# Projecting cross-attention's first queries, keys and values among self-attention's last jobs

## The chip, the cores and the metric

The kernel runs on one core of a Trainium2 chip. A core has TensorE for matrix products (PE in the profile, with its weight loads as PEld), VectorE (DVE), ScalarE (ACT), GpSimd (POOL), SyncE (SP), which here issues nearly all transfers, and 16 DMA engines. Each engine works through its own instructions in order, and semaphores order the engines among each other. The metric is the device time of one execution in microseconds. The kernel before took 792.21, 797.68 and 798.51 us in three runs, with a median of 797.68 us.

## The reference

It is a decoder layer for 8 batches of 256 tokens with 512 channels in fp32. Three sublayers follow one another, and each adds its result to its input:

```
x = x + attn(layernorm(x), w_qkv, w_out)          # 16 heads of 32 channels, causal softmax
x = x + xattn(layernorm(x), ctx, wq, wk, wv, wo)  # one head of 512 channels
x = x + ffn(layernorm(x), wg, W, b)               # 8 experts, the best one for each token

# cross-attention: the keys and values are the context and, behind it, the new tokens
q, k_new, v_new = x @ wq.T, x @ wk.T, x @ wv.T
k = concat([ctx, k_new]);  v = concat([ctx, v_new])        # 512 keys for 256 queries
out = softmax(q @ k.T / sqrt(512)) @ v @ wo.T
```

## The kernel before

**Exact products from rounded parts.** The kernel splits each fp32 operand into a high part and a low part (the rest), both in the type fp32r. A product is three passes over four chunks of 128 channels (`three_pass`, L50 to L61): high by high, low by high and high by low, so twelve matmuls. ScalarE usually writes the high part (a cast), and VectorE subtracts it from the source to get the low part. GpSimd splits some weights too.

**Three stages, one after the other.** `self_attention`, `cross_attention` and `mixture_of_experts` each open a block of their own. A block ends when all engines have finished it. Semaphores, buffers and PSUM banks of a stage belong to its block.

**Self-attention** walks over batches n = 0 to 7, and each batch has 16 slots, one for each head. Every engine has a function `slot(n, h)` with its share of slot h, and the software pipeline is written as lags: in slot h, the scores of head h are reduced, head h-1 is rounded, head h-2 is transposed by a DMA, and the values product of a group of four heads comes 7 slots after its last head. The chain of one head is: scores (PE, four heads at once), maximum (VectorE L613), shift (GpSimd L337), exponential (ScalarE L411), high part (GpSimd L344), low part (VectorE L621), DMA transpose (SP L258). Beside the heads, `SLOTS` places jobs of TensorE: X0 and X1 (transposes of the normalized input of the next batch, slot 8), y0 and y1 (the output product of the batch before, slots 10 and 11, L60 with 512 columns), q0, k0, q1, k1 of the next batch (slots 12 to 15), q2, k2, q3, k3 (slots 0 to 3), and the halves u0, u1, w0, w1 of the values (slots 4 to 7). Each job has ScalarE write the high part in its slot (L398) and VectorE the low part one slot later (L592). Jobs share three PSUM banks. For the values, VectorE writes a rest `v_rest` instead, and GpSimd makes two more parts of it (L311, L313, waits `v_mid_done` and `v_done`). In the function `values`, TensorE waits for `v_done` before the first pass of groups 0 and 2. In `evac`, VectorE waits until the rest buffer of two jobs ago is free.

There is no batch 8. So in n = 7 the slots 8 and 12 to 15 have no jobs for a next batch, and after slot 15 a tail n = 8 follows in which only lagged work is left: transposes of the last heads, the values of groups 2 and 3, then y0 and y1 for batch 7.

**Cross-attention** runs a list of jobs for each batch: `X0 X1 s0 s1 q0 q1 p0 p1 q2 q3 o0 o1 o2 o3 k0 y0 y1 k1 k2 k3 v0 Y0 Y1 v1 l0 l1` (L859), where X, q, k and v are for the next batch and the others for this one. TensorE may run up to seven PSUM banks ahead. So that batch 0 has its operands, a prologue runs first: X0 X1 q0 q1 q2 q3 k0 k1 k2 k3 v0 v1, together with the layernorm of batch 0, the split of wq and wk on ScalarE and VectorE (L1032, L1219, eight pieces each of 128 columns), the split of wv and wo on GpSimd (L986, L988) and that of the context. After the prologue TensorE waits for wo's split and for the routing constants before X0 of batch 0.

The weights of cross-attention, and its queries, keys, values and probabilities, lie in the places of the eight experts' weights, which mixture_of_experts fills at the end (`PLACES`). Self-attention has buffers of its own for all of that. wq and wk are loaded into `stage[0]` and `stage[1]` at the start of the kernel; wv, wo and the context are loaded at the start of cross-attention.

Of the kernel before, what the change touches and what calls it, by code (L numbers as in the profile page):

```python
# [20 lines left out]
P = 128  # L21
B, S, D = 8, 256, 512
DC = D // P
# [41 lines left out]
def self_attention(nc, ident, x, w_qkv, w_out, x1, xin, xr, x1_out, x1_last_out, x1_first_in,  # L65
                   stage, stage_in, next_weights):
# [8 lines left out]
    with ExitStack() as cx:  # L75
# [3 lines left out]
        w_hi, w_lo = sb("wqkv_hi", [P, DC, 3 * D], F32R), sb("wqkv_lo", [P, DC, 3 * D], F32R)  # L79
        wo_hi, wo_lo = sb("wout_hi", [P, DC, D], F32R), sb("wout_lo", [P, DC, D], F32R)  # L80
        stats, mv = sb("a_stats", [P, TB, 6]), sb("a_mv", [P, TB, 2])
        veps, rstd, expo = sb("a_veps", [P, TB]), sb("a_rstd", [P, TB]), sb("a_expo", [P, TB])
        xn = sb("a_xn", [P, TB, D])
        xt_hi, xt_lo = sb("a_xt_hi", [P, DC, S], F32R), sb("a_xt_lo", [P, DC, S], F32R)


        q_part = [sb(f"q_part{i}", [P, G, S], F32R) for i in range(2)]
        k_part = [sb(f"k_part{i}", [P, G, S], F32R) for i in range(2)]

        v_part = [sb(f"v_part{i}", [P, TB, D], BF16) for i in range(3)]  # L90
        v_rest = sb("v_rest", [P, TB, D // 2])
# [8 lines left out]
        ot_hi, ot_lo = sb("ot_hi", [P, G, S], F32R), sb("ot_lo", [P, G, S], F32R)  # L100
        raw = sb("a_raw", [P, 4, DC, D])
# [19 lines left out]
        on_done, ot_hi_done, ot_done = sem("on_done"), sem("ot_hi_done"), sem("ot_done")  # L121

# [19 lines left out]

        def piece_columns(piece):
            i = "qkuw".index(piece[0])
            if piece in "uw":
                return 2, slice(2 * D + (i - 2) * D // 2, 2 * D + (i - 1) * D // 2)
            return i, slice(i * D + int(piece[1]) * P, i * D + (int(piece[1]) + 1) * P)

        def raw_columns(piece):
            i, cols = piece_columns(piece)  # L150
            return raw[:, i, :, cols.start - i * D:cols.stop - i * D]

        def has(j, n):

            if not isinstance(n, int):
                return True
            return n >= 1 if j in LATE else n < B - 1 if j in NEXT else n < B
# [69 lines left out]
        def parts_of(j, n):  # L227

            b, i = bank(j), int(j[1])
            if j[0] == "X":  # L230
                cols = slice(i * P, (i + 1) * P)
                return xt_hi[:, :, cols], xt_lo[:, :, cols], b[:, :].rearrange("p (c n) -> p c n", c=DC)
            if j[0] in "uw":
                return v_part[0][:, i, v_half(j)], v_rest[:, i, :], b[:, 0:D // 2]
# [6 lines left out]
        def _(sp):  # L241
            sp.dma_start(xin[:], batch_rows(x, 0)).then_inc(x0_in, 16)
            for i, w in enumerate([w_qkv[:, j * D:(j + 1) * D] for j in range(3)] + [w_out]):
                sp.dma_start(raw[:, i, :, :], w.rearrange("(c p) n -> p c n", p=P)).then_inc(w_in[i], 16)
# [3 lines left out]
            for i, w in enumerate(next_weights):  # L248
                sp.dma_start(stage[i][:], w.rearrange("(c p) n -> p c n", p=P)).then_inc(stage_in[i], 16)
# [10 lines left out]

            def slot(n, h):
                if h == 13 and not (isinstance(n, int) and n in (0, B)):
                    sp.wait_ge(job_ev, job_at("y1", n) + 1)
                    sp.dma_start(batch_rows(x1, n - 1), xr[:]).then_inc(x1_out, 16)
                if h == 1 and not (isinstance(n, int) and n < 2):
                    sp.wait_ge(x1_out, (n - 1) * 16)
                    sp.dma_start(xr[:], batch_rows(x, n - 1)).then_inc(xr_in, 16)
                if h == 7 and (not isinstance(n, int) or n < B - 2):
                    sp.wait_ge(xn_ready, (n + 2) * TB)
                    sp.dma_start(xin[:], batch_rows(x, n + 2)).then_inc(x_in, 16)  # L270
                if h == 7 and isinstance(n, int) and n == B - 1:
                    sp.wait_ge(x1_out, 16)
                    sp.dma_start(xin[:], batch_rows(x1, 0)).then_inc(x1_first_in, 16)
                if head_at(h, DMA_LAG, n) is not None:
                    transpose(h, n)
# [1369 lines left out]
```

## Time and profile before

| what | value |
|---|---|
| three runs | 792.21, 797.68, 798.51 us (median 797.68) |
| the profiled execution's own time | 792.9 us |
| its span in the trace | 791.1 us |
| mean granted TensorE clock | 0.935 of full |
| busy over the span | PE 87%, DVE 63%, ACT 39%, POOL 41% |
| self-attention's block | 0 to 332.7 us |
| cross-attention's prologue | 333.5 to 363.5 us |
| cross-attention's batches | 363.5 to about 680 us |

The span is the time from the first to the last instruction in the trace. A row of the timeline has the start, the time from the first to the last of the merged instructions, the engine and line, what is written and read, how many were merged, and in brackets the idle time of the engine before it with what ended that idle time. PEclk is the granted clock as a share of the full one.

### The profile page before, as it was taken

To read this page: it belongs to the slowest core of one execution; us is meant where nothing else is said; L and a number is where in the kernel's file an instruction comes from. 1 tells how busy PE (TensorE), PEld (TensorE's weight loads), DVE (VectorE), ACT (ScalarE), POOL (GpSimd) and SP (SyncE) were. 2 spreads that over 40 slices of the span, in tenths; PEclk is the share of its full clock that TensorE was granted. 3 is DMA by queue.
4 is the path that set the end of the run, shared out by engine and by line. 5 is a ranking of instruction groups with operands and counts; after the bars stand their busy time and mean duration, and the time that the engine had idled before them with its cause. 6 is when DMAs were issued, how large, how long until landed. Compare 5 with 4: busy or idle time off the path is not lost. (4 is left out here: it accounts for less than half of the span.)

```text
span 791.1 us, 19082 instructions
## 1 busy us (share of the span) xinstructions
PE 684.9 (87%) x6040; PEld 610.1 (77%) x6041; DVE 502.4 (63%) x1454; ACT 307.1 (39%) x982; POOL 321.5 (41%) x538
## 2 busy tenths in 40 slices
PE   4769999999999995588999999999999986239995
PEld 4759888888989884487988888888888976228884
DVE  4778787877878766286645464646464557626663
ACT  3446656666656654133231222222222343102220
POOL 4396766667575756153000101010101046436662
PEclk9889999999999998679999999999999998559998
DMA  9365865766556576195312222222222046346530
GB/s 341 98 108 83 136 150 115 144 133 125 133 115 144 116 142 139 53 327 205 115 46 82 79 80 80 80 80 80 80 80 80 11 122 187 80 137 185 184 119 16
DMA packets 142885, 95.07 MB, mean 120 GB/s; under 512 B 110846, under 2 KB 115070, under 8 KB 142720
## 3 DMA queue, kind: packets, MB, share of 16 engines
q1 hardware_dynamic: 137184, 82.00, 40.7%
q0 software_dynamic: 5664, 12.61, 5.2%
q8 instruction: 19, 0.31, 0.2%
q14 instruction: 18, 0.15, 0.1%
HBM read 56.14 MB, written 18.77 MB: 95 GB/s over the span
## 5 line engine op out<-in xcount | busy, mean ns | idle before, releaser
L411 ACT ACTIVATE prob<-prob,shift 128x128 f32<-128x128 f32 (+1 forms) x256 | 114.6, 449 | 116.0 <-POOL shift L337 115.4
L60 PE MATMUL b_bank<-w_hi 128*128 128x256 f32 (+1 forms) x576 | 119.9, 331 | 7.1 <-DVE w_lo L1204 7.1
L1016 ACT CAST w_hi<-b_bank 128x256 fp32r<-128x256 f32 (+1 forms) x144 | 60.3, 446 | 160.9 <-PE b_bank L60 142.9
L60 PE MATMUL b_bank<-w_lo,w_hi 128*128 128x256 f32 (+1 forms) x576 | 114.9, 322 | 0.0
L60 PE MATMUL b_bank<-w_hi,w_lo 128*128 128x256 f32 (+1 forms) x576 | 114.6, 322 | 0.0
L60 PEld LDWEIGHTS b_bank<-w_hi 128*128 128x128 f32 x576 | 90.1, 196 | 15.6 <-DVE w_lo L1204 7.7
L613 DVE CUSTOM_DVE_ANT_0 prob<-a_s,mask 128x128 f32<-128x128 f32 (+1 forms) x256 | 79.6, 347 | 30.6 <-PE a_s L489 30.5
L1204 DVE TENSOR_TENSOR w_lo<-b_bank,w_hi 128x256 fp32r<-128x256 f32 (+1 forms) x144 | 68.3, 507 | 47.5 <-ACT w_hi L1016 47.4
L60 PEld LDWEIGHTS b_bank<-w_lo,w_hi 128*128 128x128 f32 x576 | 90.8, 195 | 8.0
L60 PEld LDWEIGHTS b_bank<-w_hi,w_lo 128*128 128x128 f32 x576 | 90.7, 194 | 7.6
L621 DVE TENSOR_TENSOR p_part<-prob,p_part 128x384 f16<-128x384 f32 x128 | 77.1, 602 | 8.2 <-POOL p_part L344 7.0
L337 POOL TENSOR_SCALAR shift<-nmax 128x2 f32<-128x2 f32 x128 | 41.6, 325 | 88.7 <-DVE nmax L613 84.9
L344 POOL CAST p_part<-prob 128x384 f16<-128x384 f32 x128 | 64.5, 504 | 8.8 <-ACT prob L411 0.7
L60 PE MATMUL a_job<-a_xt_hi,wqkv_hi 128*128 128x256 f32 x256 | 45.7, 302 | 9.4 <-DVE k_part L592 4.0
L512 PE MATMUL a_o<-pt,v_part 128*32 128x128 f16 (+1 forms) x1280 | 33.8, 254 | 20.1 <-DMA pt<-p_part 10.4
L972 POOL TENSOR_TENSOR b_rstd<-b_veps,b_expo 128x2 f32<-128x2 f32 x8 | 6.1, 758 | 109.5 <-DVE b_veps L1182 109.5
L411 ACT ACTIVATION_READ_ACCUMULATOR prob<-prob,shift 128x1 f32 x256 | 48.2, 188 | 0.0
L60 PEld LDWEIGHTS a_job<-a_xt_hi,wqkv_hi 128*128 128x128 f32 x256 | 35.6, 196 | 13.8 <-DVE k_part L592 5.6
L512 PEld LDWEIGHTS a_o<-pt,v_part 128*32 128x32 bf16 x1280 | 26.0, 99 | 25.5 <-issue 22.1
L976 POOL TENSOR_TENSOR b_rstd<-b_veps,b_expo 128x2 f32<-128x2 f32 x8 | 5.6, 699 | 95.7 <-DVE b_veps L1182 95.6
L1485 ACT CAST c_xt_hi<-c_bank 128x512 fp32r<-128x512 f32 x23 | 13.5, 588 | 74.6 <-PE c_bank L1505 74.6
L60 PE MATMUL a_job<-a_xt_lo,wqkv_hi 128*128 128x256 f32 x256 | 41.7, 287 | 0.0
(171 smaller groups left out, 1377.0 us busy)
## 6 DMA issues: line engine op xcount, KB each, us to landing
stage<-in_w SPq DMA_DIRECT2D x8, 1024.0 KB, 5.4
xin<-in_x SPq DMA_DIRECT2D x8, 512.0 KB, 4.3
xr<-in_x SPq DMA_DIRECT2D x8, 512.0 KB, 4.3
x<-xr SPq DMA_DIRECT2D x8, 512.0 KB, 3.2
xin<-x SPq DMA_DIRECT2D x8, 512.0 KB, 4.5
b_cin_t<-in_ctx_t SPq DMA_DIRECT2D x8, 512.0 KB, 3.5
b_cin<-in_ctx SPq DMA_DIRECT2D x8, 512.0 KB, 3.6
xr<-x SPq DMA_DIRECT2D x8, 512.0 KB, 4.5
```

Of the source, the lines that this page charges most:

```text
L60: ins = pe_matmul(out, a, b, start=first and i == 0, stop=last and i == len(steps) - 1)
L337: nc.gpsimd.tensor_scalar(shift[:, e, :], nmax[:, e, :], LN_UNIT, None, ALU.add).then_inc(shift_done, 1)
L344: nc.gpsimd.tensor_copy(p_part[:, t % NPROB, 0, :], prob[:, t % NPROB, :]).then_inc(p_hi_done, 1)
L411: a = nc.scalar.activation(prob[:, e % NPROB, cols], prob[:, e % NPROB, cols], ACT.Exp, scale=-1.0, bias=shift[:, e, q:q + 1], accum_out=r ...
L512: m = nc.tensor.matmul(o_ps[j * HD:(j + 1) * HD, 0, seen], v_part[a][:, k, at:at + HD], pt[:, (g * HG + j) % NPT, 3 * z + blocks.start:3 * ...
L613: m = nc.vector.tensor_tensor_reduce(out=prob[:, s % NPROB, cols], in0=s_ps[s % HG][:, q, 0:P * (q + 1)], in1=mask[:, P * (1 - q):], scale ...
L621: nc.vector.tensor_tensor(p_part[:, t % NPROB, 1, :], prob[:, t % NPROB, :], p_part[:, t % NPROB, 0, :], ALU.subtract).then_inc(p_done, 1)
L972: nc.gpsimd.tensor_tensor(rstd[:, 0, :], veps[:, 0, :], expo[:], ALU.pow).then_inc(ln_rstd, 1)
L976: nc.gpsimd.tensor_tensor(rstd[:, 1, :], veps[:, 1, :], expo[:], ALU.pow).then_inc(ln3_rstd, 1)
L1016: nc.scalar.copy(hi, src).then_inc(job_hi, 1)
L1204: nc.vector.tensor_tensor(lo, src, hi.bitcast(F32), ALU.subtract).then_inc(job_ev, 1)
L1485: nc.scalar.copy(xt_hi[:, k % 2, :], t_ps[k % 2][:, :]).then_inc(xt_hi_done, 1)
```

## The change

1. **Jobs.** The slots that were empty in n = 7 and in the tail now carry cross-attention's work for its batch 0. X0 and X1 transpose the normalized output of self-attention's batch 0. The table `CROSS` says which product stands in which slot: q0 to q3 in slots 12 to 15 of n = 7, k0 to k3 in slots 0 to 3 of the tail, v0 and v1 in slots 4 and 5 of the tail. The prologue of cross-attention is gone, and so are its waits.
2. **Weights.** wq, wk and wv are split in twelve pieces of 128 columns among the slots of n = 6 and n = 7 (`NEXT_PIECES`): ScalarE writes all high parts, GpSimd the even and VectorE the odd low parts. The context of batch 0 is split in the tail (`CTX_SLOTS`). Cross-attention splits only wo.
3. **Norms.** The layernorms of cross-attention's batches 0 and 1 are done in n = 7 and in the tail, from loads of x1 in slot 7.
4. **Places.** Self-attention's weights and operands now lie in the experts' places too: w_qkv in 3, 2 and 5, w_out in 7, queries and the transposed input in 4, keys and output in 6. Its raw weights go to the three `stage` buffers, so w_out, wk and wv are loaded in slots 2 and 3 of batch 0, behind waits, and wq in slot 0 of batch 1.
5. **Values.** `v_rest` has four places, so VectorE waits for a rest two jobs later than before. TensorE waits for `v_mid_done` before the passes, and for `v_done` only before the last pass.
6. **Loops.** VectorE, ScalarE and GpSimd leave their loop one batch earlier, and n = 6 is written out.
7. **SP.** In slot 1 the load of xr is issued after the transpose and not before it. In slot 9 of n = 7 two loads of the context stand before the transpose.

```diff
+        CROSS = {(B - 1, "q0"): "q0", (B - 1, "k0"): "q1", (B - 1, "q1"): "q2", (B - 1, "k1"): "q3", (B, "q2"): "k0",
+                 (B, "k2"): "k1", (B, "q3"): "k2", (B, "k3"): "k3", (B, "u0"): "v0", (B, "u1"): "v1"}
+        NEXT_PIECES = {**{(B - 2, 2 * i + 1): i for i in range(2 * DC)}, **{(B - 1, 2 * i + 5): 2 * DC + i for i in range(DC)}}
+        CTX_SLOTS = {(B, 0): 0, (B, 1): 1}
...
             def slot(n, h):
+                if isinstance(n, int) and (n, h) == (0, 2):
+                    sp.wait_ge(w_split, PIECES.index("q3") + 1)
+                    sp.dma_start(raw[3], chunks(w_out)).then_inc(w_in[3], 16)
+                if isinstance(n, int) and (n, h) == (0, 3):
+                    sp.wait_ge(w_split, PIECES.index("k3") + 1)
+                    load_next(1)
+                    sp.wait_ge(wv_split, 2)
+                    load_next(2)
+                if isinstance(n, int) and (n, h) == (1, 0):
+                    sp.wait_ge(wo_split, DC)
+                    load_next(0)
...
+                if h == 9 and isinstance(n, int) and n == B - 1:
+                    wait_next_split(sp, DC)
+                    sp.dma_start(ctx_t_raw, chunks(ctx_t[0:D, :])).then_inc(ctx_in, 16)
+                    sp.dma_start(ctx_raw, batch_rows(ctx, 0)).then_inc(ctx_in, 16)
...
+                i = at_slot(NEXT_PIECES, n, h - 1)
+                if i is not None and i % 2 == 0:
+                    next_low(nc.gpsimd, i)
...
-                if g == 0:
-                    pe.wait_ge(v_done, v_at("u1", of) + 1)
-                if g == G // 2:
-                    pe.wait_ge(v_done, v_at("w1", of) + 1)
+                first_use = {0: "u1", G // 2: "w1"}.get(g)
+                if first_use:
+                    pe.wait_ge(v_mid_done, v_at(first_use, of) + 1)
...
                 for a, z in PASSES:
+                    if first_use and a == 2:
+                        pe.wait_ge(v_done, v_at(first_use, of) + 1)
...
-                if j[0] in "uw":
-                    wait(dve, v_done, v_at(j, n) - 1)
+                if j[0] in "uw" and not crossed(j, n):
+                    wait(dve, v_done, v_at(j, n) - 3)
```

In cross_attention, SP and then TensorE:

```diff
-            sp.dma_start(raw[2][:], chunks(wv)).then_inc(w_in[2], 16)
-            load_ctx_t(0)
-            sp.dma_start(raw[3], chunks(wo)).then_inc(w_in[3], 16)
-            sp.dma_start(cin[:], batch_rows(ctx, 0)).then_inc(c_in, 16)
+            load_ctx_t(1)
+            sp.dma_start(wo_raw, chunks(wo)).then_inc(wo_in, 16)
+            sp.dma_start(cin[:], batch_rows(ctx, 1)).then_inc(c_in, 16)
...
-            for j in PROLOGUE:
-                job(j, -1)
-            pe.wait_ge(wg_in, 16)
-            pe.wait_ge(wo_split, 2)
-            pe.wait_ge(routing.consts, Routing.CONSTS)
```

The wait for wo's split now stands before y0 of batch 0, and those for wg and for the routing constants before its l0.

## Rows read from the trace of the kernel before

**Rows 1.** The page: busy time, share of the span and instructions of each engine.
```profile
PE 684.9 (87%) x6040; PEld 610.1 (77%) x6041; DVE 502.4 (63%) x1454; ACT 307.1 (39%) x982; POOL 321.5 (41%) x538
```
**Rows 2.** Windows: steady self-attention, its tail, the prologue, cross-attention's batch 0.
```profile
core 0: us, PE busy (x) PEld busy (x) DVE busy (x) ACT busy (x) POOL busy (x), PEclk, DMA share, GB/s
303.40:332.70 29.30, 16.73 (x181) 12.83 (x180) 10.09 (x30) 6.34 (x23) 7.96 (x16) 0.65 0.33 78
332.70:363.50 30.80, 21.43 (x128) 19.73 (x129) 25.90 (x36) 11.48 (x22) 18.43 (x18) 0.83 0.83 278
363.50:403.50 40.00, 39.74 (x256) 36.45 (x257) 20.76 (x45) 11.14 (x24) 1.40 (x2) 0.96 0.40 145
232.84:268.55 35.71, 34.12 (x449) 30.44 (x449) 28.86 (x111) 21.96 (x87) 23.46 (x50) 1.00 0.56 118
```
**Rows 3.** Timeline of the tail: last scores, values of groups 2 and 3, y.
```profile
303.40 0.96 PE L489 MATMUL a_s<-k_part,q_part 32*128 32x128 f32 x24
311.84 1.79 PE L512 MATMUL a_o<-pt,v_part 128*32 128x256 f16 x40 [5.90 <-DMA pt<-p_part]
321.03 1.22 PE L519 MATMUL a_o<-ident,rinv_wide 128*128 128x128 f32 x4
323.67 2.08 PE L60 MATMUL a_job<-wout_hi,ot_hi 128*128 128x512 f32 x4 [1.41 <-ACT ot_hi L419]
330.89 1.08 PE L60 MATMUL a_job<-wout_hi,ot_lo 128*128 128x512 f32 x4
```
**Rows 4.** Timeline: the first instruction of VectorE in the new block, X0 of batch 0.
```profile
333.69 1.28 DVE L1176 BATCH_NORM_STATS2 b_stats<-xin 128x6 f32<-128x512 f32 x2 [0.99 <-PEq L75]
363.53 1.94 PE L1105 MATMUL b_bank<-ident,b_xn 128*128 128x128 f32 x8 [2.93 <-issue]
365.12 1.89 PE L60 MATMUL b_bank<-w_hi 128*128 128x512 f32 x4
```
**Rows 5.** Timeline of one steady batch, TensorE: scores, values, X, y, scores.
```profile
232.84 0.96 PE L489 MATMUL a_s<-k_part,q_part 32*128 32x128 f32 x24
249.87 0.96 PE L489 MATMUL a_s<-k_part,q_part 32*128 32x128 f32 x24
259.08 1.09 PE L462 MATMUL a_job<-ident,a_xn 128*128 128x128 f32 x8
261.46 1.01 PE L512 MATMUL a_o<-pt,v_part 128*32 128x256 f16 x40 [1.29 <-POOL v_part L313]
262.86 1.18 PE L60 MATMUL a_job<-wout_hi,ot_hi 128*128 128x512 f32 x4
268.55 0.96 PE L489 MATMUL a_s<-k_part,q_part 32*128 32x128 f32 x24
```
**Rows 6.** TensorE's waits from 64 to 300 us: total, times, longest.
```profile
PE a_o L512 <- POOL v_part L313: 8.6, 7, 1.3
```
**Rows 7.** The same batch on GpSimd and ScalarE, around y0.
```profile
260.02 1.09 POOL L313 TENSOR_TENSOR v_part<-v_rest,v_part 128x256 bf16<-128x256 f32 x1
262.33 0.39 ACT L419 CAST ot_hi<-a_o_sb 128x256 fp32r<-128x256 f32 x1
```
**Rows 8.** By line: GpSimd's low part of 128x512 (min/median/max ns).
```profile
L321 POOL TENSOR_TENSOR wout_lo<-a_raw,wout_hi x4: 1288/1447/1466, 44.8 to 59.5; 128x512 fp32r<-128x512 f32 x4
```
**Rows 9.** Prologue: GpSimd's low part of a weight, VectorE meanwhile, L1219's min/median/max ns.
```profile
343.78 4.64 POOL L988 TENSOR_TENSOR w_lo<-stage,w_hi 128x2048 fp32r<-128x2048 f32 x1
344.51 0.43 DVE L1204 TENSOR_TENSOR w_lo<-b_bank,w_hi 128x256 fp32r<-128x256 f32 x1 [2.83 <-ACT w_hi L1016]
L1219 DVE TENSOR_TENSOR w_lo<-stage,w_hi x8: 676/681/3942, 335.4 to 350.2; 128x512 fp32r<-128x512 f32 x8
```
**Rows 10.** Batch 0 of cross-attention: the context's low part, y0; and wo's transfer.
```profile
374.37 1.22 DVE L1213 TENSOR_TENSOR w_lo<-b_cin_t,w_hi 128x1024 fp32r<-128x1024 f32 x1 [1.78 <-ACT w_hi L1026]
385.60 1.16 PE L60 MATMUL b_bank<-w_hi 128*128 128x512 f32 x4 [0.23 <-DVE w_lo L1204]
bias_sb<-in_wo SPq DMA_DIRECT2D x1, 1024.0 KB, 10.1
```

More of the change, by code:

```diff
@@ L61, in three_pass, with cross_views, self_attention @@
     return ins
-def self_attention(nc, ident, x, w_qkv, w_out, x1, xin, xr, x1_out, x1_last_out, x1_first_in,
-                   stage, stage_in, next_weights):
+CROSS_PLACES = {"q": 0, "k": 1, "v": 2, "o": 6}
+def cross_views(experts):
+    views = {n: experts.place(e) for n, e in CROSS_PLACES.items()}
+    views.update(kt=experts.place(3), xt=experts.place(4, 0, S), qt=experts.place(4, S, D), values=experts.place(5),
+                 pt=experts.place(7, 0, S), ot=experts.place(7, S, D))
+    return views
+def self_attention(nc, ident, x, w_qkv, w_out, x1, xin, xr, xn, x1_out, x1_last_out, stage, stage_in, next_weights,
+                   ctx, ctx_t, experts):
     scale = float(HD) ** -0.5
@@ L99, in self_attention @@
         o_sb = [sb(f"a_o_sb{i}", [P, S]) for i in range(2)]
-        ot_hi, ot_lo = sb("ot_hi", [P, G, S], F32R), sb("ot_lo", [P, G, S], F32R)
-        raw = sb("a_raw", [P, 4, DC, D])
+        ot_hi, ot_lo = experts.place(6, S, D)
+        raw = [stage[i][:] for i in (0, 1, 2, 0)]
+        ctx_raw = stage[0][:, 2:4, :]
+        ctx_t_raw = stage[0][:, 0:2, :].rearrange("p a n -> p (a n)").rearrange("p (c s) -> p c s", c=DC)
         job_ps = [ps(f"a_job{i}", [P, D]) for i in range(3)]
@@ L884, in route_after @@
             return "q3" if order(n) is ORDER else "p1"
[L886 to L887 removed]
         def bank(j, n):
[L890 to L893 removed]
+            return ring[order(n).index(j) % RING]
         def parts_of(j, n):
@@ L1076, in wait_bank @@
             def wait_bank(j, n):
-                before = jobs_in(n).index(j) - RING
+                before = order(n).index(j) - RING
                 if before >= 0:
-                    last, of = jobs_in(n)[before], n
-                elif isinstance(n, int) and n < 0:
+                    last, of = order(n)[before], n
+                elif isinstance(n, int) and n < 1:
                     return
@@ L1084, in wait_bank @@
                     of = n - 1
-                    there = len(jobs_in(of))
-                    last = jobs_in(of)[max(i for i in range(there) if i % RING == before + RING)]
+                    there = len(order(of))
+                    last = order(of)[max(i for i in range(there) if i % RING == before + RING)]
                 if last[0] == "s":
```

351 lines of the change are left out of this document (177 added, 174 removed).

## The prediction

> **What bounds the kernel now.** I read the busy shares first, then windows by stage, then TensorE's waits and timeline where its share falls. Over the whole span TensorE is busy 87% [rows 1], but the windows part this [rows 2]: 34.12 of 35.71 us in a steady batch of self-attention and 39.74 of 40.00 in batch 0 of cross-attention, yet only 16.73 of 29.30 in self-attention's tail and 21.43 of 30.80 in the prologue. TensorE sets the pace in the long stages. The 60 us between them go by chains, at a granted clock of 0.65 and 0.83. The timeline of the tail shows why [rows 3]: after the last scores at 303.40, TensorE waits 5.90 us for transposed probabilities, then the values come at half pace, and y0 starts at 323.67. The last of y1 ends at 331.97. The first new work of the next block starts at 333.69, and X0 of batch 0 only at 363.53 [rows 4]. So 31.6 us lie between the end of self-attention on TensorE and batch 0. The chain of waits ends in the experts' stage, which is not touched; its work follows when batch 0 starts earlier.
>
> **The prologue and the tail.** All twelve jobs leave the stretch before 363.53. Two go to slot 8 of n = 7, ten behind the last scores. To size the new tail I lay a steady batch over it. There the stretch from scores of group 3 to those of group 1 takes 249.87 - 232.84 = 17.03 us [rows 5]; it holds four jobs of the kind q and k in slots 12 to 15, values of groups 1 and 2, and four more jobs in slots 0 to 3, just what the new tail has. It also holds the scores of group 0 (0.96 us by the row of scores), which the tail has not: 16.1. The jobs v0 and v1 have 512 columns as y has: y0 and y1 together take 268.55 - 262.86 = 5.7 us, so v0 and v1 take 5.7 too. Values of group 3 take 1.4 (261.46 to 262.86). Then comes the chain from the end of the reciprocals' product to y0, 323.67 - (321.03 + 1.22) = 1.4 [rows 3], and y0 and y1, 5.7. The sum is 30.3, against 331.97 - 303.40 = 28.6 before. **The tail is only 1.7 us longer although ten jobs moved in**: they fill the wait of 5.90 and the wait for group 3, and they keep the clock up, so that the values and y0 no longer take double. Adding the 1.7 us from the last matmul to the next block (331.97 to 333.69), X0 of batch 0 would start at 331.97 + 1.7 + 1.7 = 335.4 in place of 363.53: **-28.1 us**.
>
> For this the transposed probabilities must be there in time. Before, group 2's came at 311.84 and group 3's before the reciprocals' product at 321.03 [rows 3]; TensorE would now ask for them about 12 and 22 us after the last scores, at 315 and 325. They are hidden. What is late next is the evacuation of the jobs: three banks, ScalarE and VectorE also with the context's parts (two of 1.22 us on VectorE [rows 10]) and a norm. VectorE was busy 10.09 us of the 29.30 in the tail [rows 2] and gets about 9 more (ten low parts of 0.43 [rows 9] or above, the context's 2.4, the norm as an estimate 2.5). I take **+1**, with bounds 0 and +4 (all three new large pieces of about 1.3 us in front of one evacuation).
>
> X0 and X1 in slot 8 of n = 7 cost 1.1 us. In steady batches TensorE waits there for the values' parts anyway, 8.6 us in 7 times [rows 6]. I put them at nothing; without that cover they would cost 1.1.
>
> **The clock at batch 0.** X0 and X1 ran 1.94 us and the first four matmuls of s0 1.89, after an idle time of 2.93 [rows 4]; at the full clock the same shapes take 1.09 and 1.08 [rows 3, 5] (the row of X, and the last four matmuls of y1). In the new kernel TensorE pauses about 1.7 us. An idle time of 1.29 in the steady batch left y0 at full pace [rows 5]. That row is nearer: **-1.7**, bounds -1.7 and 0.
>
> **Splitting twelve pieces during n = 6 and n = 7.** ScalarE has 13.8 us idle in a batch, VectorE 6.9, GpSimd 12.3 [rows 2]. GpSimd gets six low parts of 1.45 us [rows 8], VectorE six of 0.68 [rows 9]. Over a batch this fits. But one piece of GpSimd falls in slot 6 of each of the two batches, among the values' parts, and GpSimd's order there leads to y0: the second part of u1 (260.02 to 261.11), then the shift of head 8, the exponential, ot_hi (262.33 to 262.72), y0 at 262.86 [rows 5, 7]. The slack is 0.14 us, so each piece there costs 1.3. The others meet idle time of GpSimd, but can hold VectorE. I take **+3** (twice 1.3, and 0.4), bounds 0 and +8 (all six at 1.45 in the path, 8.7, less some).
>
> **The values' waits.** The edit takes away nearly all of the 8.6 us [rows 6], since `v_mid_done` comes 1.09 us before `v_done`. It would be -8.6 if nothing else came last. But y0, which follows, waits for ot_hi, and that ends 0.14 us before y0 starts [rows 5, 7]; GpSimd's work ahead of it is unchanged. So a wait for ot_hi takes the place of the one removed. Seven times 0.14 is **-1**; bounds -9.6 (all eight waits, the one in batch 0 with them) and +1 (the second wait between passes).
>
> **Batch 0 of cross-attention.** y0 comes 385.60 - 363.53 = 22.1 us after X0 [rows 10, 4]. wo's transfer landed 10.1 us after its issue [rows 10] with 1 MB more ahead of it, which at the prologue's 278 GB/s [rows 2] is 3.8 us; GpSimd's low part takes 4.64 [rows 9], its cast by my estimate half of that, and the issue comes some 2 us into the block: 2 + 10.1 - 3.8 + 2.3 + 4.6 = 15.2, or 19 without the 3.8. y0 is covered. The danger is GpSimd's low part itself. In the prologue GpSimd's first one ran from 343.78 to 348.42. VectorE's low parts of weight pieces, from SBUF like it, took 0.68 us in the middle and once 3.94, in that time; one with a source in PSUM took only 0.43 [rows 9]. Before, that fell in the prologue. Now it starts some 10 to 14 us after X0, and the context's low part starts 10.8 us after X0 [rows 10]; the low parts of q and p queue behind it on VectorE, and o0 waits for p's. If it loses, o0 is 4 us late. The Trainium skill ("SBUF — State Buffer", section "SBUF: two separate sides") says that VectorE with two SBUF inputs and GpSimd take a shared port pair as an exclusive lock for a whole instruction, the first one winning. The trace agrees (3.94 us). I take half, **+2**, bounds 0 and +4.6.
>
> **The start.** w_out, wk and wv (3 MB) leave the kernel's first transfers and come in slots 2 and 3, wk and wv ahead of the transposes of heads 1 to 3 on SP's queue. Their 2 MB take some 7 us by the prologue's 278 GB/s [rows 2], so some transposes can land up to 7 us late; the values of their group stand in slot 10, five slots on. w_out's first piece was split at about 44 us [rows 8], long after slot 2. The Trainium skill ("DMA: Bandwidth & Descriptors", "Queues, rings and completion order") has each DMA engine take its descriptors in ring order; that rule would put the whole 7 us in front of the transposes, and the sum would then be 4 us higher if GpSimd had to wait for the buffers. I take **+1**, bounds -1 and +5. The new places, the written-out batch and the later xr load I put at nothing: cross-attention's matmuls already read the same places with TensorE busy 39.74 of 40.00 us [rows 2], and xr is needed only in slot 10.
>
> **The sum**: -28.1 + 1 - 1.7 + 3 - 1 + 2 + 1 = -23.8. The profiled execution took 792.9 us, so 769.1. The runs' median is 797.68, 4.8 above this execution, and the lowest run 0.7 below; I forecast **770**.
>
> **Rivals.** *The values' waits come off whole*: if the order of parts lets ot_hi move up with them, self-attention is another 7.6 us shorter, 761.5. For it speaks that VectorE no longer stalls twice a batch on the same parts; against it the 0.14 us. Chance 0.16. *The locks spread*: the six pieces of GpSimd stop it and VectorE one after the other (2 x 1.45 x 6 = 17.4 in place of 3), and batch 0 loses 4.6 in place of 2: 769.1 + 14.4 + 2.6 = 786. Against it is the idle time of both engines. By the SBUF page's lock this is the outcome when GpSimd always wins; the one row that shows it has a POOL instruction three times as long. Chance 0.12. *Nothing is hidden in the tail* (the change doesn't do what it says): the evacuations and the context make the ten jobs follow one another behind the last values. Their work, eight of 1.4 and 5.7, is 17 us, in place of 1.7 and 1: 769.1 + 14.3 = 783. Against it are the 12.6 us that TensorE idles there [rows 2]. Chance 0.08. *Slower*: the wait between the passes. TensorE now holds inside `values` until GpSimd's last part, in every batch, while VectorE, freed of its waits, takes the shared ports from GpSimd with its p_part instructions. If each of the eight batches loses 3.6 us or more, the 28.8 lost are more than the 28.6 between 769.1 and the median, and at 5 us it is 809. For it speaks that the part already takes 1.09 us [rows 7] beside VectorE, against it that it would have to take four times as long. Chance 0.03.
>
> **How the numbers follow.** The forecast has 0.61. Its own range is 762 to 777. For 8 in 10 I take in the first rival with what the unknown costs allow below and most of the second and third: 757 to 785. A change under 1% (8 us) can't be told from none here. Faster by over 1% (under 789.7) is the forecast, the first rival, and most of the second and third: 0.92. Within 1%: the upper ends of those two, 0.05. Slower: 0.03.
>
> **What would show it.** In the changed profile, X0 of cross-attention's batch 0 should start at about 333 to 340 us, with PEclk near 1 in the tail and no wait for transposed probabilities over 1 us. The last scores of n = 7 should come at 303 to 308. The wait for L313 should be gone and one for ot_hi stand there, at the same period of 35.7 us. Batch 0 should take 38 to 43 us, with a VectorE instruction of about 4 us beside GpSimd's low part if the lock is met. I am wrong if the steady period moves by over 1 us, or if the tail is over 36 us long.

## The result

The changed kernel took **762.08 us** (median of 4 runs, 761.97 to 764.43) beside 797.98 us (792.21 to 798.51) for the kernel before: a ratio of 0.957, with a 95% interval of 0.953 to 0.962 (intervals stand behind the ratios below too). Run again later it took 761.31 us beside 789.24, a ratio of 0.965 (0.962 to 0.969); the two intervals hardly touch, and the difference lies in the kernel before, whose median was 789.2 to 790.6 us in the three later sets of runs. Both are faster, and both agree on the kernel after. The forecast was 770, range 757 to 785. The drop is 36 us in the first set and 28 in the second. The two profiled executions differ by 28.4 us in their spans (791.1 and 762.7), and it is these 28.4 us that can be followed place by place. The executions themselves took 792.9 and 764.43.

The page of the kernel after: the span, busy time by engine, and the granted clock in 40 slices.

```profile
span 762.7 us, 18978 instructions
PE 677.9 (89%) x6040; PEld 604.5 (79%) x6041; DVE 497.5 (65%) x1452; ACT 309.2 (41%) x986; POOL 322.2 (42%) x542
PEclk9969999999999999999999999999999988559998
```

TensorE's work is nearly what it was [rows 1], and its share rose by two points because the span shrank. The hole of low clock between the two stages is gone. Its own windows, which answer to [rows 2], are the new tail, batch 0 of cross-attention, and a steady batch of self-attention (columns as there):

```profile
312.31:342.70 30.39, 28.78 (x301) 25.04 (x300) 18.30 (x49) 13.24 (x40) 12.58 (x21) 1.00 0.38 81
...
344.38:383.20 38.82, 38.28 (x256) 35.13 (x257) 22.91 (x44) 11.03 (x24) 10.83 (x16) 1.00 0.90 316
201.11:236.86 35.75, 34.80 (x449) 30.97 (x449) 29.09 (x111) 22.00 (x87) 23.18 (x50) 1.00 0.61 132
```

The tail now keeps TensorE busy for 28.78 of 30.39 us at the full clock, where it had 16.73 of 29.30 at 0.65. Its timeline answers to [rows 3] and [rows 4]:

```profile
316.27 1.01 PE L632 MATMUL a_o<-pt,v_part 128*32 128x256 f16 x40
...
324.07 1.01 PE L632 MATMUL a_o<-pt,v_part 128*32 128x256 f16 x40
...
333.99 1.01 PE L632 MATMUL a_o<-pt,v_part 128*32 128x256 f16 x40
334.93 0.71 PE L639 MATMUL a_o<-ident,rinv_wide 128*128 128x128 f32 x4
337.06 1.20 PE L60 MATMUL a_job<-w_hi 128*128 128x512 f32 x4 [1.41 <-ACT w_hi L516]
...
344.38 1.06 PE L1190 MATMUL b_bank<-ident,xn 128*128 128x128 f32 x8 [1.59 <-PEq L89]
345.19 1.17 PE L60 MATMUL b_bank<-w_hi 128*128 128x512 f32 x4
```

No values product waits for transposed probabilities any more, each takes 1.01 us in place of 1.79, and X0 of the next block takes 1.06 in place of 1.94. The only wait over 1 us in the tail is the one for the rounded output (w_hi of L516 is `ot_hi`) ahead of y0, 1.41 us, the same as before.

**Where the 28.4 us are.** I read the start of the last scores (group 3) of each batch of self-attention, and of X0 of each batch of cross-attention, in both timelines, and took differences:

| stretch | before | after | difference | forecast |
|---|---|---|---|---|
| start to last scores of n = 0 | 48.69 | 52.66 | +3.97 | +1 |
| n = 1 to 5 | 184.15 | 184.20 | +0.05 | -1 (seven waits) |
| n = 6 and 7 | 70.56 | 75.45 | +4.89 | +3 |
| last scores to X0 of batch 0 | 60.13 | 32.07 | -28.06 | -27.1 |
| batch 0 | 40.03 | 38.82 | -1.21 | +0.3 (-1.7 and +2) |
| X0 of batch 1 to X0 of batch 6 (five periods) | 201.06 | 191.41 | **-9.65** | 0 |
| after the last X0 | 186.48 | 188.09 | +1.61 | 0 |

The sum is -28.40. The forecast of -23.8 is near it, but two errors cancel in part: a gain of 9.65 us that it did not have at all, and 4.9 us more loss at the start and in n = 6 and 7 than it had. With the missed gain left out, the change made the execution 18.75 us shorter and not 23.8.

Each column is one execution. The places before cross-attention hang on it by about 1 us: in the mirror experiment below, self-attention's code is that of the kernel before, and its last scores of n = 0 came at 49.34 us in place of 48.69 and its batches 1 to 5 took 183.00 in place of 184.15, a steady period of 35.50 and not 35.71. Differences under about 1 us in the table mean nothing by themselves.

### The profile page after: what moved, and what is told of

Read it like the earlier page. It is cut to its first block and busy times, and to the rows that moved or that the text cites. A ratio compares the mean times of both kernels' runs of the same rounds, so it can differ in the third digit from the quotient of the medians.

```text
span 762.7 us, 18978 instructions
## 1 busy us (share of the span) xinstructions
PE 677.9 (89%) x6040; PEld 604.5 (79%) x6041; DVE 497.5 (65%) x1452; ACT 309.2 (41%) x986; POOL 322.2 (42%) x542
## 5 line engine op out<-in xcount | busy, mean ns | idle before, releaser
L60 PE MATMUL b_bank<-w_hi 128*128 128x256 f32 (+1 forms) x536 | 109.7, 327 | 3.2 <-DVE w_lo L1281 3.2
L60 PE MATMUL a_job<-w_hi 128*128 128x256 f32 (+1 forms) x488 | 94.5, 317 | 15.0 <-DVE w_lo L711 7.2
L60 PE MATMUL b_bank<-w_hi,w_lo 128*128 128x256 f32 (+1 forms) x536 | 106.8, 322 | 0.0
L60 PE MATMUL b_bank<-w_lo,w_hi 128*128 128x256 f32 (+1 forms) x536 | 106.7, 322 | 0.0
L60 PEld LDWEIGHTS a_job<-w_hi 128*128 128x128 f32 x488 | 71.3, 195 | 24.8 <-DVE w_lo L711 7.8
L60 PE MATMUL a_job<-w_lo,w_hi 128*128 128x256 f32 (+1 forms) x488 | 87.7, 303 | 0.0
L60 PE MATMUL a_job<-w_hi,w_lo 128*128 128x256 f32 (+1 forms) x488 | 87.1, 301 | 0.0
L60 PEld LDWEIGHTS a_job<-w_lo,w_hi 128*128 128x128 f32 x488 | 72.3, 195 | 3.0
L60 PEld LDWEIGHTS a_job<-w_hi,w_lo 128*128 128x128 f32 x488 | 72.2, 195 | 2.9
L711 DVE TENSOR_TENSOR w_lo<-a_job,w_hi 128x256 fp32r<-128x256 f32 (+1 forms) x92 | 43.2, 477 | 18.8 <-ACT w_hi L495 18.4
```

Of the source, the lines that this page charges most:

```text
L60: ins = pe_matmul(out, a, b, start=first and i == 0, stop=last and i == len(steps) - 1)
L711: nc.vector.tensor_tensor(lo, src, hi, ALU.subtract).then_inc(job_ev, 1)
```

## The experiments

### The gain that was not forecast: the order of two loads

The edit puts back the order in which SyncE issues its loads in a batch of cross-attention:

```diff
                 if load:
+                    sp.wait_ge(ct_split, n + 1)
+                    load_ctx_t(n + 2)
                     if not (isinstance(n, int) and n == 0):
                         sp.wait_ge(xn_ready, n * TB)
                         sp.dma_start(xin[:], batch_rows(x1, n + 2)).then_inc(x_in, 16)
-                    sp.wait_ge(ct_split, n + 1)
-                    load_ctx_t(n + 2)
```

> The changed kernel with one thing put back: in cross-attention's batches, SP again issues the load of the next-but-one x1 rows (xin) behind the load of the transposed context and not ahead of it. Theory A (VectorE's wait for xin set 1.5 us of each cross-attention batch): X0 to X0 goes from 38.3 to about 39.75 us in batches 1 to 5, VectorE shows waits of 3.2 us for xin again, and TensorE waits before the ranks; in all 7 to 11 us longer, about 771. Rival B (the cross-attention batches became shorter for another reason, the places or the time at which the experts' weights arrive): 762 to 764, and X0 to X0 stays at 38.3.

It took 772.34 us (ratio 0.978, 0.974 to 0.982). The mirror experiment makes the same edit, turned round, in the kernel before, and nothing else:

```diff
-                    sp.wait_ge(ct_split, n + 2)
-                    load_ctx_t(n + 2)
                     sp.wait_ge(xn_ready, (n + 2) * TB)
                     sp.dma_start(xin[:], batch_rows(x1, n + 2)).then_inc(x_in, 16)
+                    sp.wait_ge(ct_split, n + 2)
+                    load_ctx_t(n + 2)
```

> The kernel before with that one part of the change alone: SP issues the xin load of a cross-attention batch ahead of the wait for the context's split. Theory A: the batches fall from 39.75 to about 38.3 us, batch 1 with its 41.8 by more, in all 8 to 11 us, so 788 against 798. Rival B: no change, 796 to 799.

It took 780.82 us beside 790.48 for the kernel before, 9.7 less (ratio 0.988, 0.983 to 0.992). The five periods from X0 of batch 1 to X0 of batch 6 sum to 201.31 us with the late load in the changed kernel and to 191.27 us with the early one in the kernel before; the two kernels themselves have 201.06 and 191.41. So the order of the loads carries the 9.65 us whole, in either kernel, and the rest of the change none of it.

The rows show how. First the kernel before, SyncE's queue in one batch, then VectorE in the same batch:

```profile
495.88 0.37 SPq L914 DMA_DIRECT2D b_cin_t<-in_ctx_t  x1
496.51 0.37 SPq L945 DMA_DIRECT2D xin<-x  x1
```

```profile
494.48 1.23 DVE L1213 TENSOR_TENSOR w_lo<-b_cin_t,w_hi 128x1024 fp32r<-128x1024 f32 x1 [1.78 <-ACT w_hi L1026]
...
500.86 1.29 DVE L1176 BATCH_NORM_STATS2 b_stats<-xin 128x6 f32<-128x512 f32 x2 [3.22 <-DMA xin<-x]
```

The load of xin stands behind a wait for VectorE's split of the context (494.48 to 495.71). It is issued at 496.51 and wanted by VectorE only a little later: VectorE stands for 3.22 us, and the low parts behind it stand too. In the kernel after, SyncE has already issued xin when it comes to that wait, and VectorE's row has no wait:

```profile
472.21 1.27 DVE L1256 BATCH_NORM_STATS2 b_stats<-xin 128x6 f32<-128x512 f32 x2
```

What TensorE waits for from X0 of batch 0 to the end, before and after (total us, times, longest; the experts' stage and its DMA left out):

```profile
PE b_bank L60 <- DVE w_lo L1204: 5.8, 7, 1.6
PE r_ranks L731 <- DVE r_onehot L716: 5.1, 6, 1.8
```

```profile
PE b_bank L60 <- DVE w_lo L1281: 3.2, 3, 1.6
...
PE r_ranks L857 <- DVE r_onehot L842: 1.7, 1, 1.7
```

VectorE was busy 22.09 of 39.75 us in such a batch, and still set 1.5 us of it, by one wait. Of these 1.5 us TensorE spent 1.05 waiting; for the other 0.4 it was busy longer with the same 263 matmuls. In the kernel before, two batches in a row (X0 to X0 of batch 1, and of batch 2), and one of the kernel after:

```profile
403.56:445.37 41.81, 40.04 (x263) 36.69 (x263) 22.14 (x58) 10.85 (x25) 3.58 (x4) 0.96 0.26 76
...
445.37:485.12 39.75, 38.70 (x263) 35.33 (x263) 22.09 (x58) 10.85 (x25) 3.87 (x6) 1.00 0.24 79
```

```profile
421.49:459.76 38.27, 38.27 (x263) 35.25 (x263) 22.31 (x58) 11.13 (x25) 3.86 (x6) 1.00 0.38 83
```

TensorE no longer waits in such a batch. In batch 1 of the kernel before the waits came with a clock of 0.96, which made its work 1.3 us longer besides.

### The start: bulk loads ahead of the transposes

In the kernel after, GpSimd waits for a transpose in batch 0, which it never did before, and SyncE's queue shows what stood ahead of it (the second fence: start, length, what was issued):

```profile
POOL p_part L426 <- DMA pt<-p_part: 4.1, 1, 4.1
```

```profile
31.84 0.57 SPq L324 DMA_DIRECT2D stage<-in_wk  x1
32.46 0.51 SPq L324 DMA_DIRECT2D stage<-in_wv  x1
33.08 9.49 SPq L320 DMA_TRANSPOSE pt<-p_part  x4
```

The experiment moves both loads into batch 1:

```diff
-                if isinstance(n, int) and (n, h) == (0, 3):
+                if isinstance(n, int) and (n, h) == (1, 5):
                     sp.wait_ge(w_split, PIECES.index("k3") + 1)
                     load_next(1)
+                if isinstance(n, int) and (n, h) == (1, 9):
                     sp.wait_ge(wv_split, 2)
                     load_next(2)
```

> The changed kernel with the loads of wk and wv moved from slot 3 of batch 0 to slots 5 and 9 of batch 1. Theory A (the 4 us lost at the start are GpSimd's wait of 4.1 us for transposes that stand behind these 2 MB): the last scores of batch 0 come at 48.7 and not 52.7 us, and 758 in all. Rival B (the start is late because the splits come from other buffers or w_out lands late): the scores stay at 52 to 53 us, 762. Rival C (the 2 MB cost the same wherever they stand): 762, with the 4 us lost in batch 1.

It took 759.64 us (ratio 0.961, 0.957 to 0.965; the kernel after has 0.957 and 0.965 in its two sets of runs). The last scores of batch 0 came at 48.78 in place of 52.66, so the start's loss is due to these two loads. But those of batch 1 came at 93.30 in place of 93.91: batch 1 took 44.52 us in place of 41.25. TensorE's waits in that batch show the load's cost again, in a new place:

```profile
PE a_s L609 <- issue: 5.2, 3, 4.4
PE a_o L633 <- DMA pt<-p_part: 2.9, 1, 2.9
...
```

In this execution the third theory held: the transfers cost about the same in batch 1 as in batch 0. But it took 761.91 us, the longest of the four runs; the others took 758.05 to 759.71, between the first theory's 758 and the third's 762, and have no trace. So how often the cost comes back is not shown, and the last kernel below shows that it need not.

### Batches 6 and 7: does the place of the pieces matter?

```diff
-        NEXT_PIECES = {**{(B - 2, 2 * i + 1): i for i in range(2 * DC)}, **{(B - 1, 2 * i + 5): 2 * DC + i for i in range(DC)}}
+        NEXT_PIECES = {**{(B - 2, h): i for i, h in enumerate((1, 3, 4, 6, 8, 10, 12, 14))},
+                       **{(B - 1, h): 2 * DC + i for i, h in enumerate((4, 6, 8, 11))}}
```

> The changed kernel with the twelve weight pieces at other slots: GpSimd's now fall in slots 2, 5, 9 and 13 of n = 6 and 5 and 9 of n = 7, and no longer in slots 6 and 10, where it also makes the values' parts. Theory A (a piece costs about 1.3 us where GpSimd's parts lead to y0, and nothing elsewhere): of the 4.9 us that n = 6 and n = 7 lost, 2 to 3 come back, 759 to 760. Rival B (the cost is the shared work on all engines, wherever it stands): 761 to 763.

It took 760.34 us (ratio 0.962, 0.958 to 0.966). Batches 6 and 7 took 38.66 and 37.26 us, 75.92 together, against 75.45 in the kernel after (75.45 to 75.50 in the five executions whose n = 6 and 7 have the code of the kernel after). My theory, that two pieces in slot 6 of GpSimd cost 1.3 us each and the others next to nothing, is refuted. In both kernels the loss is about 5 us, and in both TensorE waits for GpSimd's first part of the values (L394, L395) again, which it does not do in the steady batches of the kernel after. Here are the waits, the kernel after first:

```profile
PE a_o L632 <- POOL v_part L394: 2.5, 2, 1.4
PE a_job L60 <- ACT w_hi L516: 2.2, 2, 1.1
```

```profile
PE a_o L633 <- POOL v_part L395: 2.7, 2, 1.9
PE a_job L60 <- DVE w_lo L712: 1.0, 2, 0.8
PE a_job L60 <- ACT w_hi L517: 0.6, 1, 0.6
```

Not all of the 4.9 us is waiting. TensorE was busy 70.07 us of these 75.45, and 67.50 of 70.56 before: 2.6 us are longer work, 2.3 are waits. About 0.9 of the work is X0 and X1: n = 7 took 34.85 us before, without them, where a batch with them takes 35.71 [rows 2]. Most of the rest is an effect that the steady batches show too: 449 matmuls keep TensorE busy 34.80 us there in place of 34.12 [rows 2], and steady batches hide it in their waits (next section). The waits are not tied to a slot of the pieces. No run leaves the pieces out, and n = 7 also got the norms and loads for cross-attention, so that the waits come from the pieces at all is argued and not shown.

### The values' waits: what gives them back

```diff
                 if first_use:
-                    pe.wait_ge(v_mid_done, v_at(first_use, of) + 1)
+                    pe.wait_ge(v_done, v_at(first_use, of) + 1)
...
-                    if first_use and a == 2:
-                        pe.wait_ge(v_done, v_at(first_use, of) + 1)
```

> The changed kernel with TensorE waiting for v_done ahead of the first pass again. Theory A (y0 is bound by ot_hi, so the earlier start of the values product gives nothing): the period of self-attention stays at 35.7 us, the wait of 0.7 us for ot_hi before y0 goes away and one of about 1.3 us for the values' last part comes back; the same time as the changed kernel. Rival B (the new wait did gain, and something else in the change cost as much): 35.7 becomes 36.5 or more, and 5 to 8 us more in all.

It took 761.7 us (ratio 0.964, 0.960 to 0.967), the same as the kernel after, with the same period of 35.7 us. The wait for the values' last part came back at 0.8 us and not the 1.3 expected; the mirror experiment, with the old self-attention, has 0.9. In n = 6 and 7 alone the old wait cost something, 76.15 us in place of 75.45. The next kernel leaves TensorE's waits as changed and moves ScalarE's rounding of the output ahead of the exponential of the same slot:

```diff
             def slot(n, h):
+                g = group_at(h, OT_HI_LAG, n)
+                if g is not None:
+                    ...
+                    nc.scalar.copy(ot_hi[:, g, :], o_sb[g % 2][:]).then_inc(ot_hi_done, 1)
                 e = head_at(h, 0, n)
...
                     a.then_inc(ex_done, 1)
-                g = group_at(h, OT_HI_LAG, n)
-                ...
```

> The changed kernel with ScalarE writing ot_hi ahead of the exponential in each slot and not behind it. Theory A (ScalarE's order, exponential of head 8 and then ot_hi, binds y0, so that the wait for the values' parts was worth nothing by itself): y0 starts 0.7 us earlier in each batch, the period of self-attention falls from 35.7 to about 35.0, 5 us less in all than the changed kernel. Rival B (GpSimd's chain behind it is the bound, ot_lo takes the place of ot_hi): the same time. Rival C (the exponential is late instead): 2 us more or worse.

It took **755.8 us** (ratio 0.957, 0.954 to 0.960), with a period of 35.17 us. And both edits together, the early rounding with the old waits:

> ot_hi ahead of the exponential, and v_done ahead of the first pass, both in the changed kernel. Theory A (both waits must go for a gain): the time of the changed kernel, period 35.7 us. Rival B (the order on ScalarE alone gives the gain): 5 us less than the changed kernel.

It took 760.25 us (ratio 0.962, 0.958 to 0.965), with a period of 35.58. TensorE's waits over four steady batches of each (after, then old wait, then early rounding, then both):

```profile
PE a_job L60 <- ACT w_hi L516: 2.7, 4, 0.7
PE a_job L60 <- DVE w_lo L711: 1.0, 4, 0.2
```

```profile
PE a_o L630 <- POOL v_part L396: 3.1, 4, 0.8
...
```

```profile
PE a_job L60 <- DVE w_lo L711: 1.0, 4, 0.2
```

```profile
PE a_o L630 <- POOL v_part L396: 3.2, 4, 0.8
...
```

The kernel with the old wait alone has a period of 35.73 us. From there the changed wait alone gives nothing (35.74), the early rounding alone 0.15, and both 0.56 (35.17): each edit alone leaves one of two waits of about 0.7 us a batch. The period is 35.73 to 35.74 us in each of the seven traced kernels that have the late rounding and the rest of the change, so 0.56 is clear; the 0.15 is smaller than the 0.2 us between two executions of the old self-attention. This is the forecast's reading of [rows 5] and [rows 7], now shown for the changed kernel: ot_hi took the place of the wait removed, because ScalarE came to it only after an exponential that had stood 0.91 us for its shift. ScalarE in the kernel after, ahead of y0 at 231.18:

```profile
229.78 0.40 ACT L508 ACTIVATE prob<-prob,shift 128x128 f32<-128x128 f32 x1 [0.91 <-POOL shift L419]
...
230.67 0.39 ACT L516 CAST w_hi<-a_o_sb 128x256 fp32r<-128x256 f32 x1
```

With both waits gone the period is TensorE's work (busy 34.82 us of 35.15 in one such batch), and that work grew by the change. From the last scores of a batch to the scores of group 2 in the next, TensorE took 25.35 us before, 0.30 of it waiting, and 25.73 in the kernel after, 0.24 of it waiting, with the same matmuls at the full clock: 0.44 us more. (Busy time grew by 0.68, as it also counts to its end a matmul that a wait now follows.) Two low passes of a job and the scores of group 2, before (after the last scores at 232.84) and after (after those at 201.11):

```profile
234.30 0.62 PE L60 MATMUL a_job<-a_xt_lo,wqkv_hi 128*128 128x256 f32 x4
234.75 0.62 PE L60 MATMUL a_job<-a_xt_hi,wqkv_lo 128*128 128x256 f32 x4
...
258.19 0.96 PE L489 MATMUL a_s<-k_part,q_part 32*128 32x128 f32 x24
```

```profile
202.58 0.64 PE L60 MATMUL a_job<-w_lo,w_hi 128*128 128x256 f32 x4
203.06 0.64 PE L60 MATMUL a_job<-w_hi,w_lo 128*128 128x256 f32 x4
...
226.84 0.33 PE L608 MATMUL a_s<-w_hi 32*128 32x128 f32 x4
```

Such passes come 0.48 us apart in place of 0.45. Which part of the change does this, the new places of the operands or another, no run separates; the forecast put the places at nothing. While the waits stand, it costs nothing in a steady batch.

### The tail: is it TensorE's work?

This kernel makes only the first pass (high by high) of the six jobs in the tail, cross-attention's k0 to k3, v0 and v1:

```diff
-                    if kind == "v":
+                    if n == B:
+                        for c in chunks:
+                            pair = (xt_hi[:, c, toks], wt_hi[:, c, :]) if kind == "v" else (wt_hi[:, c, toks], xt_hi[:, c, :])
+                            m = nc.tensor.matmul(b[:, :] if kind == "v" else b[:, 0:S], *pair, start=c == 0, stop=c == DC - 1)
+                    elif kind == "v":
```

> The changed kernel with part of the computation left out: the six jobs k0 to k3, v0 and v1 of the tail are one pass (high by high) in place of three. That takes 4 x 0.95 + 2 x 1.85 = 7.5 us of work from TensorE between the last scores and y0. Theory A (the jobs fill time in which TensorE would otherwise wait for the last heads' transposed probabilities, and keep its clock up): the tail from the last scores to X0, 32.1 us, gets only 1 to 4 us shorter, a wait for pt comes back, and the granted clock of the tail falls. Rival B (the jobs are added time): the tail is 7.5 us shorter.

It took 758.52 us (two runs; ratio 0.960, 0.956 to 0.964). The tail from the last scores (311.01) to X0 (340.38) took 29.37 us in place of 32.07: 2.7 us shorter for 7.5 us less work by the expectation, of which 5.1 show in TensorE's busy time (23.71 in place of 28.78), since part of what is left ran slower. The wait for transposed probabilities that theory A expected did not come; TensorE waits for evacuations instead, the clock falls, and the values of group 3 come at half pace again:

```profile
311.01:340.38 29.37, 23.71 (x254) 19.14 (x253) 18.75 (x50) 12.76 (x40) 12.39 (x22) 0.94 0.40 83
```

```profile
PE a_job L577 <- DVE w_lo L715: 2.5, 3, 1.4
```

```profile
328.86 1.79 PE L636 MATMUL a_o<-pt,v_part 128*32 128x256 f16 x40
```

So the tail of the kernel after lies near balance: its length is TensorE's work plus 1.6 us of waits, and 7.5 us less of that work won only 2.7.

### Together, on one chip

The kernel after was run once more beside two others: the early rounding again, and all three edits (early rounding, loads in batch 1, pieces moved).

> The changed kernel itself, unaltered, beside the two below on one chip, so that their differences don't rest on runs of other chips. Every theory: a ratio of 0.955 to 0.963 to the kernel before, last scores of batches 0 to 7 within 0.3 us of 52.66, 93.91, 129.65, 165.39, 201.11, 236.86, 274.65, 312.31, cross-attention's batches 38.3 us long. If these places move by more than 1 us between two runs of one kernel, the smaller differences of this study (the pieces, the loads) say nothing.

> The changed kernel with ScalarE's ot_hi ahead of the exponential, once more, beside the unaltered one. A: the gain is real: 5 to 7 us less than the changed kernel on the same chip, period 35.17 in place of 35.74. B: it was the chip: within 2 us of it, though the period stays 35.17.

> ot_hi ahead of the exponential, the loads of wk and wv in slots 5 and 9 of batch 1, and the pieces away from the values' parts. A: what loads and pieces cost is a fixed amount of work on engines near their limit, so it only changes places: 755 to 757 us, within 1.5 us of ot_hi first alone, last scores of batch 1 at 92 to 93 again. B: once ot_hi is out of the way the engines have slack, and the three add up: the start loses its 3 us and batches 6 and 7 about 2 more, so 750 to 752 us with last scores of n = 7 at 302 to 304.

| kernel | median, us | range | ratio to before |
|---|---|---|---|
| after | 761.31 | 760.64 to 762.76 | 0.965 (0.962 to 0.969) |
| early rounding | 755.97 | 755.65 to 756.84 | 0.958 (0.955 to 0.962) |
| all three | 753.14 | 752.23 to 754.64 | 0.955 (0.952 to 0.959) |

The early rounding is worth 5.3 us again. The three together beat both kernels and took 753.14 us, 2.8 under the early rounding alone, which falls between what the two theories had. The places tell which edit gave it: last scores of batch 0 at 48.74 (52.55 with early rounding alone), of batch 1 at 89.24 (92.79), so this time batch 1 did not give the 3.6 us back; batches 6 and 7 took 74.02 us in place of 73.35, so moving the pieces again gave nothing. TensorE's wait for the transposes in batch 1 was 0.6 us here, and 2.9 with the loads alone:

```profile
PE a_o L634 <- DMA pt<-p_part: 0.6, 1, 0.6
```

So both theories on the loads were too simple. That the transfers find room between the transposes once the engines are a little ahead is my reading; what decides it was not tried, and with one trace each the two kernels may also differ by chance.

The kernel after, run twice, has its places within 1.0 us of each other (last scores of n = 7 at 312.31 and 311.32, X0 of batch 0 at 344.38 and 343.36), not within the 0.3 expected. Nearly all of that arises before the last scores of n = 1. The periods of self-attention behind them agree within 0.03 us, so that small differences of periods can be read and small differences of places can't. The second execution has 185.6 us for the last stretch, after the last X0, where the first has 188.09. The 1.61 us of the table's last row are therefore within what one kernel does by itself.

## Why the prediction was right, step by step

- **The tail.** Forecast 30.3 us and 1.7 to the next block, plus 1 for evacuations; measured 30.48 and 1.59 (312.31 to 342.79, where the last matmul ends, to 344.38), with TensorE waiting 0.2 us for an evacuation. Right within 1 us, and by its own mechanism: laying a steady batch over the slots that were to be filled. Its terms hold one by one: values of group 3 start 21.68 us behind the last scores (forecast 16.1 + 5.7 = 21.8), y0 3.07 behind that (forecast 2.8), y0 and y1 take 5.7. The +1 was not needed.
- **The clock at batch 0.** Forecast -1.7. X0 and X1 took 1.06 in place of 1.94 us, and the first four matmuls of s0 1.17 in place of 1.89: 1.6 us. Right.
- **The values' waits.** Forecast -1, with ot_hi in their place at the same period. Right in its reading, and shown by the two edits, 0 and 0.15 us a batch alone and 0.56 together. The 0.14 us a batch that it did count on is too small to be seen. The first rival (761.5 us, the waits come off whole) has the time that was measured, and is refuted: the waits gave nothing in a steady batch. That its time was met is luck.
- **Batch 0 and the port lock.** Forecast +2, a VectorE instruction of about 4 us. It came, but elsewhere. Rows of GpSimd, VectorE and TensorE in batch 0 of the kernel after:

```profile
356.79 4.62 POOL L1095 TENSOR_TENSOR w_lo<-bias_sb,w_hi 128x2048 fp32r<-128x2048 f32 x1
```

```profile
353.73 1.23 DVE L1290 TENSOR_TENSOR w_lo<-b_cin_t,w_hi 128x1024 fp32r<-128x1024 f32 x1 [1.78 <-ACT w_hi L1130]
...
356.80 1.27 DVE L1256 BATCH_NORM_STATS2 b_stats<-xin 128x6 f32<-128x512 f32 x2
357.99 0.41 DVE L1260 BATCH_NORM_AGGREGATE b_mv<-b_stats 128x2 f32<-128x6 f32 x2
358.43 3.29 DVE L1262 TENSOR_SCALAR b_veps<-b_mv 128x2 f32<-128x2 f32 x1
```

```profile
365.26 1.16 PE L60 MATMUL b_bank<-w_hi 128*128 128x512 f32 x4 [0.54 <-DVE w_lo L1281]
```

  The context's low part was through 1.8 us before GpSimd's began. Held instead was an addition on 128x2 elements, 3.29 us where it takes 0.17 otherwise; the next VectorE instruction began at 361.35, where GpSimd's ended (361.41); the statistics just ahead of it, beside the same GpSimd instruction, were not held. Behind it stood low parts for TensorE, and TensorE waited 0.54 us for one at y0, where it had waited 0.23 before [rows 10]. The step had the collision right, but not the instruction that it would stop nor the size: about +0.3 in place of +2. TensorE may run ahead by several banks, and the trace shows no more of the 3.1 us reaching it. The Trainium skill ("SBUF — State Buffer", section "SBUF: two separate sides") says that VectorE takes the shared pair in a two-port mode or with two SBUF inputs, and then waits for the whole of a GpSimd instruction that began first. The addition has one SBUF input, so by that rule it ran in such a mode; that fits with the rows, which show no mode.
- **The pieces.** Forecast +3 by two places of GpSimd, measured +4.9, of which 0.9 is X0 and X1, put at nothing, and part of the rest is TensorE's longer work, which the forecast did not have either. The size was near by luck; the reason given for it is refuted by the moved pieces.
- **The start.** Forecast +1, measured +4.0 (2.6 to 4.0 over all the traces in which the start has the code of one or the other kernel). The bounds of -1 to +5 held it, and the step chose wrongly inside them. GpSimd did wait for a transpose, 4.1 us. The step had written that the outcome would be 4 us higher in that case, and set it aside because the values stand five slots on; what counted was not the values but the buffers that GpSimd wants back. The Trainium skill's rule on ring order ("DMA: Bandwidth & Descriptors", "Queues, rings and completion order"), named there, pointed to this result, and the wait of 4.1 us agrees with it.
- **What was missing.** The diff moves one load of SyncE above a wait in cross-attention's batch, and the forecast has no term for it: -9.65 us. The profile of before showed a price for it, the 3.22 us of VectorE in a steady batch quoted above; it was not looked for because TensorE was busy 39.74 of 40.00 us in batch 0 [rows 2]. VectorE stood for xin in batch 0 too, 3.2 us once, but TensorE's longer waits begin in batch 1: that batch has 40.04 us of work in 41.81, the next 38.70 in 39.75. The forecast had taken the one batch in which nothing was to be seen for the stage.

The kernel with the late load, which is the changed kernel without that gain, took 772.34 us; the forecast was 770. The measured median lies 8 us below the forecast, and the place for it is a line that the forecast passed over.

Of the signs that the prediction named, the steady period, the tail under 36 us, its clock near 1, the wait for ot_hi in the place of the one for L313, and batch 0 at 38.8 us came true. Two did not: the last scores of n = 7 came at 312.31 and not at 303 to 308, and X0 of batch 0 at 344.38 and not at 333 to 340. By X0 of batch 0 the kernel after was only 19.15 us ahead of the kernel before, where the forecast's terms up to there give 24.1; the missed gain behind it made up for that and more. That the total came out so near owes something to luck. The tail, which carries most of the change, does not.

## What to carry to other kernels

When work is to be moved into idle slots, find a stretch of the same kernel in which these slots are already full, and lay it over them: that gave the tail's 30.48 us to 0.2. Read a stage in a steady batch and not in its first one, and give each line that a diff moves in a queue its own question: what did it stand behind, and who waits for it? A wait that is removed is worth what is left to the next arrival, so look for the second wait and move both; here 0 and 0.15 us alone became 0.56 us a batch together.

## What the runs showed of the hardware

- An addition on 128x2 elements took 3.29 us in place of 0.17 beside GpSimd's subtraction of 128x2048, while batch-norm statistics did not stretch beside the same one (1.27 us for two; 1.29 without it). In the kernel before a low part read from PSUM did not stretch beside such a subtraction either (0.43 us) [rows 9].
- Two loads of 1 MB each ahead of four transposes on SyncE's queue made GpSimd wait 4.1 us for a buffer (3.6 in a second execution). The same loads ahead of transposes of another batch made TensorE wait 2.9 us in one kernel and 0.6 in another.
- An idle time of 1.59 us behind the tail, which ran at a granted clock of 1.00, left the next matmuls at full pace (1.06 us for eight transposes). Behind the prologue, which ran at a mean of 0.83 and ended in an idle time of 2.93 us, they took 1.94 us [rows 4]. Which of the two differences matters is not shown.
